# The order in which the query scores of the long attention take the four heads of a group

## What is computed

```python
Q, K, V = (proj(w_q), proj(w_k), proj(w_v))          # 16 heads of 8 dimensions
scores = jnp.einsum('bhqd,bhkd->bhqk', Q, K) / jnp.sqrt(jnp.float32(D_K))
attn = jax.nn.softmax(scores, axis=-1)
out = jnp.einsum('bhqk,bhkd->bhqd', attn, V)
out = out.transpose(0, 2, 1, 3).reshape(B, S, D)
out = jnp.einsum('bsd,ed->bse', out, w_o) + b_o
return _layer_norm(x + out, ln_g, ln_b)
```

## Time and profile before

| | |
|---|---|
| median of three runs | 4202.99 us (4201.47 to 4204.4) |
| the profiled execution's own time | 4212.23 us |
| its span in the trace | 4210.4 us |
| slots 0 to 256 of the long attention in the trace | 3618 to 4095 us |
| busy over the span | PE 92%, DVE 80%, ACT 65%, POOL 50% |
| mean granted TensorE clock | 0.955 of 2.4 GHz |

### The profile page before, as it was taken

The page is one execution under the profiler, slowest core; times in us unless marked ns, Lnnn a source line. Parts: engine busy times, 40 slices in busy tenths (PEclk is TensorE's granted clock), DMA queues, the critical chain, the costliest instruction groups (busy, mean ns, idle before and its releaser), DMA issues.

```text
span 4210.4 us, 151591 instructions
## 1 busy us (share of the span) xinstructions
PE 3890.2 (92%) x65521; PEld 2419.1 (57%) x65521; DVE 3375.6 (80%) x6704; ACT 2737.0 (65%) x4940; POOL 2092.4 (50%) x1202
## 2 busy tenths in 40 slices
PE   6999999999999998589999999999999986999985
PEld 3666666666666666456666666666666654333333
DVE  7988888888888888588888888888888875677735
ACT  4767767777677676167777676777767752366652
POOL 4756656566666665066566565665656630000000
PEclk9999999999999999799999999999999998699977
DMA  3112121121121211112121211212111110000000
GB/s 101 40 34 55 41 53 39 38 58 35 39 55 40 55 35 41 25 28 44 32 58 40 55 35 40 55 42 52 40 39 35 35 31 1 1 1 1 1 1 10
DMA packets 131142, 153.71 MB, mean 37 GB/s; under 512 B 67480, under 2 KB 90408, under 8 KB 128816
## 3 DMA queue, kind: packets, MB, share of 16 engines
q1 hardware_dynamic: 130480, 144.02, 15.0%
HBM read 35.93 MB, written 1.05 MB: 9 GB/s over the span
## 4 chain that ended last, share of the span: by engine, by line
PE 63%; DVE 24%; issue 7%; ACT 4%; POOL 0%; DVEq 0%; SPq 0%; POOLq 0%; DMA 0%; ACTq 0%
PE psum L377 10%; DVE turn L670 9%; PE psum L446 8%; PE psum L388 8%; PE psum L413 6%; DVE den L752 5%; PE psum L438 4%; DVE nmax L730 4%; PE psum L366 3%; PE psum L1292 3%; PE psum L459 3%; PE psum L1280 3%; PE psum L466 3%; PE psum L476 3%; PE psum L1282 2%
## 5 line engine op out<-in xcount | busy, mean ns | idle before, releaser
L670 DVE TENSOR_TENSOR turn<-psum,ropes 128x512 f32<-128x512 f32 x1536 | 938.7, 673 | 6.6 <-POOL qkr L801 4.2
L808 POOL TENSOR_TENSOR turn<-turn 128x1024 f32<-128x1024 f32 x384 | 903.5, 2374 | 25.5 <-DVE turn L670 25.5
L551 ACT ACTIVATE sq<-psum 128x512 f32<-128x512 f32 x768 | 456.0, 594 | 543.4 <-PE psum L366 543.4
L820 POOL TENSOR_TENSOR scratch<-scratch,rden 128x1024 f32<-128x1024 f32 x192 | 365.6, 1904 | 879.5 <-DVE rden L755 879.5
L366 PE MATMUL psum<-wqkv,xT 128*128 128x512 f32 x1536 | 771.8, 625 | 32.4 <-DVE turn L670 30.6
L801 POOL TENSOR_TENSOR qkr<-turn,rn 128x1024 f32<-128x1024 f32 x384 | 728.5, 1919 | 19.6 <-DVE rn L691 19.4
L388 PEld LDWEIGHTS psum<-ident,qkr 128*128 128x128 f32 x3072 | 334.9, 143 | 342.7 <-issue 160.9
L377 PE MATMUL psum<-wqkv,xT 128*64 128x512 f32 x1536 | 431.2, 641 | 62.7 <-DVE turn L670 50.7
L388 PE MATMUL psum<-ident,qkr 128*128 128x128 f32 x3072 | 473.0, 288 | 5.7 <-POOL qkr L801 5.1
L696 DVE TENSOR_REDUCE ss<-sq 128x16 f32<-128x1024 f32 x384 | 448.4, 1209 | 0.0
L425 PEld LDWEIGHTS psum<-scratch,Vs 64*64 64x64 f32 (+1 forms) x12288 | 326.5, 134 | 183.4 <-issue 181.1
(11 more groups left out here) (191 smaller groups left out, 6416.7 us busy)
## 6 DMA issues: line engine op xcount, KB each, us to landing
Vs<-V SPq DMA_DIRECT2D x384, 128.0 KB
Vs<-V SPq DMA_DIRECT2D x768, 64.0 KB
wqkv<-in_L_ffn_Wqkv_dram SPq DMA_DIRECT2D x12, 1536.0 KB
wo<-in_L_ffn_Wo_dram SPq DMA_DIRECT2D x48, 128.0 KB
zs<-Y SPq DMA_DIRECT2D x192, 31.8 KB
w<-in_L_ffn_W_dram SPq DMA_DIRECT2D x12, 341.0 KB
zs<-Y SPq DMA_DIRECT2D x168, 0.2 KB
w<-in_L_ffn_W_dram SPq DMA_DIRECT2D x12, 128.0 KB
```

The costliest lines, as they stand in the source:

```text
L551: act.activation(sq[:, q // 2, q % 2, :, :], bank[QK_BANK[q]][:, :].rearrange("p (h d) -> p h d", d=RH), ACT.Square).then_inc(sem("squared ...
L670: e = dve.tensor_tensor(dst, src, tab.unsqueeze(1).broadcast_to([P, HEADS, RH]), ALU.mult)
L808: pool.tensor_tensor(t1, t1, turn2[:, w, :, :, :].rearrange("p a h d -> p (a h d)"), ALU.add).then_inc(sem("added"), 1)
```

## The change

The heads of four consecutive units are taken in the order 0, 2, 1, 3. The position of a unit in the program, its banks, its semaphores and its counts stay; only the 32 partitions that it reads, and the column of at_max, are those of another head.

```diff
+        UNIT_ROWS = (0, 2, 1, 3)
...
             def scores2(u):
-                n, t, r = u // 32, u // 4 % 8, u % 4
+                n, t, r = u // 32, u // 4 % 8, UNIT_ROWS[u % 4]
...
                 u = max_unit(j)
                 if u is not None:
-                    i, c, b = u // 16, P * (u // 4 % 4) + 32 * (u % 4), S2_BANK[u % 2]
+                    i, c, b = u // 16, P * (u // 4 % 4) + 32 * UNIT_ROWS[u % 4], S2_BANK[u % 2]
```

## The result

The changed kernel takes 4229.56 us, the median of 16 runs that lie between 4206.89 and 4241.66; 16 runs of the kernel before, taken beside them, have a median of 4204.02 and lie between 4201.28 and 4206.47. The ratio is 1.0057, with a 95% interval from 1.0045 to 1.0069: 0.6% slower, where 0.05% had been forecast. The prediction was wrong. Its range ended at 4211. The profiled execution took 4230.92 us by its own time, 18.7 more than that of before.

A forecast was written before the change was run, and what follows sets the result against it. The prediction took a ring of key tiles and ScalarE's exponentials to bound the kernel. Four kinds of slot at 0 plus six late projections, 2.2 us, on the median of 4202.99 gave 4205.2 us, range 4199 to 4211.

The forecast's parts named there:

- The wait on ScalarE bounds the turn: Two slots of the long attention, batch to batch, take 3.05 us, set by key tiles waiting for ScalarE's exponentials.
- slots 0 and 3 modulo 4: Slots whose heads stay 0 and 3 as before; claimed cost 0.
- Slots 2 modulo 4: Scores move to row 1, delaying the second key tile's maximum 0.46 us; covered by ScalarE's queue, cost 0.
- The projections of slot 27: Projections behind slots 26 of every 32 start 0.36 us late, passed on whole in six groups: 2.2 us.
- Slots 1 modulo 4: Scores move to row 2, free 0.46 us earlier, but row 0's chain of four keeps the array occupied; gain 0.
- The clock: Rival: the edit shifts a rise or fall of the granted clock; over 8.4 us: 2% faster, 3% slower.
- a turn or two: Size of the clock shift in that rival: two turns at 1.83 us more each at the lower clock, 3.7 us.
- The argument against it: Against the clock rival: the number of matmuls and of their rows is the same in each four slots.
- The prediction's own sign of being wrong: Turn without projection changed over 0.1 us, 0.36 missing behind slot 93, or 0.50 stretches differing by over a few microseconds.
- The faster rival: Spreading scores over rows in slots 1 modulo 4 gains 27.1 us, giving 4178.1 us; chance 1%.

The follow-up runs named there:

- e3: Kernel before, with the new head order only in slots 24 to 27 of every 32, where the projections begin; 4232.65 us, ratio 1.0038.
- e6: Kernel before, its own head order, with the two score matmuls of slot 26 of every 32 issued twice; 4226.61 us, ratio 1.0061.
- e2: Kernel before, with the new head order only in slots 4 to 7 of every 32, around the turned sums; 4213.59 us, ratio 0.9999.
- e14: Changed kernel, with the score matmuls of slot 5 of every 32 issued three times and those of slot 21 twice; 4195.12 us, ratio 0.9949.
- e17: Changed kernel, with e14's repeated score matmuls only from the second group on; 4198.61 us, ratio 0.9976.
- e5: Changed kernel, with the old head order kept in slots 24 to 27 of every 32, where projections begin; 4193.93 us, ratio 0.9972.
- e12: The same program as e5, run again on another chip against the kernel before; 4223.41 us, ratio 1.0010.
- e9: Changed kernel, with VectorE's two additions two slots later in each group, at slots 6 and 8 of 32; 4202.35 us, ratio 0.9995.
- e16: Kernel before, with e14's repeated score matmuls and two unread score matmuls more in each of slots 238 to 255; 4192.34 us, ratio 0.9954.

## Why the prediction was wrong

- **The wait on ScalarE bounds the turn; slots 0 and 3 modulo 4 cost nothing.** Right. The turn is 3.04 to 3.05 us in the new profile too.
- **Slots 2 modulo 4: the delayed key tile is covered.** Right. It starts 0.23 us behind the second score matmul, and the turn around it is as long as before.
- **The projections of slot 27: 0.36 us late, passed on whole.** Right as a time: 0.77 us behind the second score matmul instead of 0.42, and e3's and e6's groups without a fall last 58.21 to 58.27 us against 57.88. What failed was to take it for all that the change costs.
- **Slots 1 modulo 4: "the array is occupied until the same moment".** Wrong in slots 5 and 21 of 32. The transposes split row 0's chain there, and the releaser isn't ScalarE but VectorE. The row that shows it for slot 5 was in the trace, with 0.33 us of idle time; I had checked the slots with the maxima and carried the finding over. In time this step was harmless, as e2 shows.
- **The clock, put at nothing in the sum.** This is the step that failed. The sum has no term for the clock; the six falls made six groups 41.6 us longer, of which the late projections explain 2.2, and 23.8 us of it came back elsewhere, 16.0 in the rest of the stage and 7.8 behind it. The clock stood among the rivals, with 5%, 3% of it for slower. Two things in that rival were mis-sized. It let a rise or fall shift "by a turn or two", 3.7 us; a fall cost 6.6 us (a group of 64.8 us against the 58.2 of e3), and came once in each of six groups. And it let such a shift move a rise or a fall that was there, not bring new ones. The runs show otherwise: in e3 and e6, 0.36 us a group brought a fall of 44.4 us. My explanation is that a long fall comes only where the clock's own moment meets the idle time behind the turned sums, and that 0.36 us a group, added up, walks the stage into that place, or past it. The argument against it, "the number of matmuls is the same in each four slots", was beside the point, as e6 lost the clock with more matmuls. That the kernel before already had one such fall, at 4011.4, was visible as a gap between two lines of rows 2, and I priced it nowhere. The prediction's own sign of being wrong, stretches at 0.50 of another length, is what came.
- **The rule of the Trainium skill.** The Trainium skill, "TensorE: Matmul & The Clock Gate", section on the HAM clock gate, has the clock drop after idleness. The long falls do come behind idle time, of 0.30 to 0.78 us, and with the idle time filled the profiles of e14 and e17 have none; so idle time does count. But with 0.78 us in slot 37 of e2 and e5 the clock stayed up in their profiles, and eight short falls came with no idle time; the length of the idle time alone decides nothing here. The prediction had worked out that by the rule this edit would change nothing in the clock, 4205.2, and had kept the rival's chance. The six falls speak against that use of the rule.
- **The faster rival.** The Trainium skill, "TensorEngine Tiling (Array Packing)", section Key Properties, has tiles work independently of each other. The batches shown agree, with matmuls on different rows starting together at 3801.10 and 3721.22; it is worth nothing here, as forecast.

What stays open: why the distance is 1.24 to 1.69 us, and what the short falls need; why the same program (e5 and e12) has most runs near 4194 on one chip and near 4224 on another; and why a long fall lasts 17.1, 23.9 or 44.4 us. That groups longer by 0.36 us are enough to bring long falls is shown by e3 and e6, on two chips, each with one such fall in its profile. That they need the idle time is supported by all thirty and by the times of e14 to e17, of which only one, of e17, lies above 4202, at 4219.04. That the added-up shift decides is my reading of the profiled runs. Eight runs of e12 and five of e9 lie above 4221 without longer groups, and the place of the groups in each single run wasn't measured.

## What to carry to other kernels

A stage whose granted clock moves between its two levels has no small shifts: before an edit there is costed at a fraction of a microsecond, list the places at which TensorE idles in each period and the falls that are there already, and price one fall in each period, as a row of falls can repeat itself. If such a place is found, fill it with matmuls that nobody waits for; that took 0.24% off this kernel in e17 and 0.43 to 0.51% in e14 to e16, which all ran on one chip. With the row of falls gone, the order of the heads made no difference that could be told. And a time from one chip is not enough for a version whose gain hangs on the clock: run it again elsewhere, and look at the scatter of the runs, not at the median alone. The filled versions e14 to e16 still need that.

## What the runs showed of the hardware

- Matmuls on different rows of the array start out of program order. In slot 108 the second score matmul of row 0 stands ahead of the slot's two key tiles in the program and starts at 3822.06. Three key tiles start around it, one of slot 107 and the two of slot 108, at 3821.72, 3821.74 and 3822.29; so at least one of slot 108 started before it. The Trainium skill, "TensorE: Matmul & The Clock Gate", section on packing small matmuls, has matmuls start and end in the order of the program; in this kernel's traces they don't. Nothing in these rows needs another order than the program's within one array row. Timeline of PE, kernel before:

```profile
3821.72 0.49 PE L1280 MATMUL psum<-qst,kst 32*128 32x512 f32 x1
...
3821.74 0.49 PE L1280 MATMUL psum<-qst,kst 32*128 32x512 f32 x1
```

- On one array row the starts are 0.23 us apart at the higher clock, 0.33 to 0.34 behind the first of a batch, and 0.42 to 0.43 at the lower clock. Matmuls on other rows of the array run beside them at the same steps, and a matmul for the whole array starts 0.32 us behind the last of a row.
- In the six falls TensorE shows as busy all the time at 1.2 GHz, for 17.10 of 17.10 us in the first, while it idled about 3 of 47.7 us at 2.4 GHz in the stretches between. Busy time in the profile doesn't tell which level will be granted next.
